# The expert stage of an attention and mixture-of-experts kernel: loops written out, two more row buffers, no copies of the index column

## The chip, the cores and the metric

The kernel runs on one core of one Trainium2 chip. The metric is the time of one execution on the device in microseconds (us), the median of several runs.

## What is computed

The reference takes `x` of shape (2, 1024, 256) and a context of shape (2, 154, 256), and makes two residual steps:

```python
x = x + attention(layernorm(x), ctx, Wq, Wkv, Wout, bout)      # 16 heads, causal past the context
x = x + ffn(layernorm(x), Wg, W1, W2)

def ffn(x, Wg, W1, W2):            # xt: 2048 tokens x 256, E = 8 experts, F = 512
    probs = softmax(xt @ Wg)
    top_idx = top_k(probs.T, T // E)          # each expert picks 256 tokens
    tok2exp = ...                             # one expert for each token
    weights = probs of that expert
    for e in range(E):
        gate = where(tok2exp == e, weights, 0)
        out = out + gate[:, None] * (gelu(xt @ W1[e]) @ W2[e])
```

Each token ends with exactly one expert, so the second step needs one pass of 2048 tokens through weights that depend on the token.

## The kernel before, in words

Five engines run programs of their own and meet at semaphores. Up to about 282 us the kernel does projections, attention and the gate's logits. Then the routing (282 to 326 us) finds each token's expert and sorts the tokens by expert into tiles of 128 slots. A tile holds tokens of one expert only, so some slots stay empty. Three tables say what is where: `slot_tok` [128, 24], column k of which holds the token numbers of tile k (a number past the last token for an empty slot); `slot_gate`, the weights; `r_texp`, the expert of each tile. 20 tiles (`NS_MOST`) are always done; 4 more only if the routing needed them (`more`), in a branch at the end of each engine's program.

The expert stage, which the change touches, does for each tile k:

1. GpSimd (POOL), `take`: an indirect DMA gathers 128 rows of `rows_d` (`token_rows` in the profile) by the token numbers into a row buffer `xs_sb` (part of the tensor `mid`). A row holds the normalised token (256 floats) and the residual (256 floats). There are `RING` = 4 row buffers, and one semaphore `xs_in` for each.
2. TensorE (PE), `ffn_xt`: two transposes of the normalised half to PSUM. ScalarE (ACT), `ffn_x`, copies them to SBUF.
3. ACT, `ffn_w`: reads the expert number from `r_texp` into a register and copies that expert's first-layer weights to one of two fixed buffers (`w1c_sb`, inside `piece_f`). PE, `ffn_w1`: 8 matmuls (16 records in the trace), first layer. ACT, `ffn_h`: gelu.
4. PE, `ffn_w2`: reads the expert number into a register of its own and does 4 matmuls (8 records) straight from the expert's second-layer weights, `w2_sb`.
5. VectorE (DVE), `ffn_y`: times the gate, plus the residual, into one of 4 buffers `y_sb`.
6. POOL, `give`: an indirect DMA scatters the 128 rows to `out`.

Called X(k) for `ffn_xt`, W1(k), W2(k), y(k), and take(k), give(k) below, the order on PE is X(0), W1(0), X(1), and then W1(k+1), X(k+2), W2(k) for each k. The order on POOL is the first four takes; then, when y(k) is done, take(k+4) into the buffer that y(k) has just read, and give(k). PE, ACT, DVE and POOL each run this as a hardware loop (`Fori`) whose body does four tiles. In a loop the column number k is a register, and the index operand of an indirect DMA is a fixed column, so POOL first copies column k to a small tensor with a `tensor_tensor` add of zero and waits for it on the semaphore `took`:

```python
nc.gpsimd.tensor_tensor(take_ix[u][:, :], slot_tok[:, bass.ds(k, 1)], zero1[:, :], ALU.add).then_inc(took, 1)
pool.wait_ge(took, at)
```

Of the kernel before, what the change touches and what calls it, by code (L numbers as in the profile page):

```python
# [44 lines left out]
RING = 4  # L45
NST = 3
# [63 lines left out]
def xattn_ffn(nc, x, ctx, Wq, Wkv, Wout, bout, Wg, W1, W2, out, rows_d, qd, kd, sums_d, recs_d, force_shift=False):  # L110
# [13 lines left out]
    with es:  # L124
# [107 lines left out]
        xs_in = [sem(f"xs_in{i}") for i in range(RING)]  # L232
# [75 lines left out]
        took = sem("took")  # L308
# [67 lines left out]
        xs_sb = [work(XW) for _ in range(RING)]  # L376
# [225 lines left out]
        def _(pool):  # L602
# [31 lines left out]
            nc.gpsimd.memset(zero1[:, :], 0).then_inc(tri_made, 1)  # L634
# [55 lines left out]
            def give(u, k, at):  # L690

                pool.wait_ge(fy_done, k + 1 + 2)
                nc.gpsimd.tensor_tensor(give_ix[u][:, :], slot_tok[:, bass.ds(k, 1)], zero1[:, :], ALU.add).then_inc(took, 1)  # L693
                pool.wait_ge(took, at)
                pool.sem_inc(index_there, 1)
                pool.indirect_dma_start(out_rows, bass.IndirectOffsetOnAxis(give_ix[u][:, :], 0), y_sb[u], None,  # L696
                                        bounds_check=T - 1, oob_is_err=False).then_inc(sent[u], 16)

            for u in range(RING):
                take(u, u, u + 1)  # L700
            for u in range(RING):
                pool.wait_ge(fy_done, u + 1 + 2)
                take(u, RING + u, RING + 2 * u + 1)
                give(u, u, RING + 2 * u + 2)
            with pool.Fori(1, NS_MOST // RING - 1) as it:
                for u in range(RING):
# [4 lines left out]
            at = 2 * NS_MOST - RING  # L711
            for u in range(RING):
                pool.wait_ge(sent[u], 16 * (NS_MOST // RING - 1))
                give(u, NS_MOST - RING + u, at + u + 1)
            pool.wait_ge(texp_done, 2)
            fl = pool.value_load(more[0:1, 0:1], min_val=0, max_val=1)
            with pool.If(fl > 0):
                with pool.Fori(NS_MOST // RING, NS // RING) as it:
                    for u in range(RING):
                        take(u, it * RING + u, it * (2 * RING) + u + 1)  # L720
                    for u in range(RING):
                        pool.wait_ge(sent[u], it * 16)
                        give(u, it * RING + u, it * (2 * RING) + RING + u + 1)
# [3 lines left out]
        def _(act):  # L727
# [135 lines left out]
            def ffn_w(pa, k):  # L863

                e = act.value_load(r_texp[0:1, bass.ds(k, 1)], min_val=0, max_val=E - 1)
                act.wait_ge(fh_ready, k + 1)
                nc.scalar.copy(w1c_sb[pa], w1_sb[:, bass.ds(e * (KT * F), KT * F)]).then_inc(fw_done, 1)  # L867

            def ffn_x(pa, k):
                act.wait_ge(fx_ready, k + 1)  # L870
                act.wait_ge(fh_ready, k + 1)
                nc.scalar.copy(xT_sb[pa], bank(pa)[:, 0:D]).then_inc(fx_done, 1)  # L872

            def ffn_h(pa, k):
                act.wait_ge(fh_ready, k + 1 + 2)
                act.wait_ge(fy_ready, k + 1)
                nc.scalar.activation(hT_sb[pa], bank(2 + pa), ACT.Gelu).then_inc(fg_done, 1)  # L877

            def tiles(k, last):
                for u in range(RING):  # L880
                    nxt = u < RING - 1 or not last
                    if nxt:
                        ffn_w((u + 1) % 2, k + u + 1)
                    ffn_h(u % 2, k + u)
                    if nxt:
                        ffn_x((u + 1) % 2, k + u + 1)

            ffn_w(0, 0)
            ffn_x(0, 0)
            with act.Fori(0, NS_MOST // RING - 1) as it:  # L890
                tiles(it * RING, False)
            tiles(NS_MOST - RING, True)
            fl = act.value_load(more[0:1, 0:1], min_val=0, max_val=1)
            with act.If(fl > 0):
                with act.Fori(NS_MOST // RING, NS // RING) as it:
                    ffn_w(0, it * RING)
                    ffn_x(0, it * RING)
                    tiles(it * RING, True)
# [3 lines left out]
        def _(pe):  # L902
# [276 lines left out]
            def ffn_xt(u, k, nth):  # L1179
# [546 lines left out]
```

## Time and profile before

| | |
|---|---|
| median of 3 runs | 428.44 us (428.04 to 429.25) |
| the profiled execution, its own time | 426.05 us |
| its span in the trace | 424.2 us |
| PE busy in the span | 359.4 us (85%) |
| ACT, DVE, POOL busy | 259.4, 208.5, 118.9 us |
| expert stage, first weight copy to last row out | about 327 to 424 us |

The span is what the trace covers; the execution's own time is 1.85 us longer. Engine time is counted as busy only while an instruction works; loading registers, branching and waiting is not. An indirect DMA on POOL is shown as busy for the time in which its descriptors are made; the data lands later.

### The profile page before, as it was taken

The page shows a single profiled execution, that of the slowest core. Times are in us where ns is not written, and L with a number is a line of the kernel's source. Part 1 is how long each engine was busy: PE and PEld are TensorE (multiplying, and loading weights), DVE is VectorE, ACT ScalarE, POOL GpSimd, SP SyncE. Part 2 cuts the span into 40 slices and gives each one's busy share as a digit, 9 for nine tenths or more (in the row PEclk, how much of TensorE's full clock was granted, in tenths as well). Part 3 has the DMA queues.
Part 4 walks back from the last instruction along what each step waited for, and adds up shares of the span by engine and source line. Part 5 has one row for each costly group of instructions (what it writes and reads, how often), then busy time and mean ns, then how long its engine had stood idle before and what let it go on. Part 6 is the DMA issues. An engine that isn't in the chain of part 4 may idle for free.

```text
span 424.2 us, 10996 instructions
## 1 busy us (share of the span) xinstructions
PE 359.4 (85%) x4207; PEld 232.5 (55%) x4208; DVE 208.5 (49%) x785; ACT 259.4 (61%) x354; POOL 118.9 (28%) x175
## 2 busy tenths in 40 slices
PE   2989898999999999999999999841139799989893
PEld 1646456445343545453435468830039788879782
DVE  5849973745373646363646558358877010101010
ACT  1456456899999999999999925430000444444430
POOL 4244789300030303030302100000001345555543
PEclk9999999899999999999999999555559999999999
DMA  8325995304494446434842352800000322222210
GB/s 271 97 102 154 275 272 167 125 4 101 112 258 113 105 117 201 118 98 126 235 122 39 94 182 96 287 15 1 0 2 2 93 64 76 65 81 68 76 50 26
DMA packets 36760, 47.61 MB, mean 112 GB/s; under 512 B 8460, under 2 KB 25794, under 8 KB 36705
## 3 DMA queue, kind: packets, MB, share of 16 engines
q1 hardware_dynamic: 33808, 40.26, 33.2%
q0 software_dynamic: 2560, 6.30, 5.0%
q8 instruction: 35, 0.57, 0.6%
q10 hardware_dynamic: 337, 0.32, 0.2%
q14 instruction: 20, 0.16, 0.1%
HBM read 32.71 MB, written 13.81 MB: 110 GB/s over the span
## 4 chain that ended last, share of the span: by engine, by line
PE 63%; DVE 13%; ACT 9%; DMA 6%; issue 5%; SPq 2%; POOL 1%; POOLq 0%; ACTq 0%; DVEq 0%
PE ps L1002 15%; PE ps L981 14%; PE ps L966 7%; PE ps L1204 7%; PE ps L1194 7%; ACT pbuf L790 6%; PE ps L950 4%; DVE v_st L1581 3%; PE ps L1091 2%; PE ps L1065 2%; DMA pbuf<-in_L_xattn_Wkv 2%; DMA mid<-token_rows,take_ix 2%; DMA sums<-mid 2%; PE ps L1082 1%; SPq L491 1%
## 5 line engine op out<-in xcount | busy, mean ns | idle before, releaser
L790 ACT ACTIVATE pbuf<-ps 128x1024 f32<-128x1024 f32 (+3 forms) x192 | 169.3, 1030 | 3.6 <-PE ps L981 3.5
L1454 DVE SCALAR_TENSOR_TENSOR pbuf<-pbuf,seen 128x128 f32<-128x128 f32 (+2 forms) x288 | 79.2, 317 | 64.1 <-ACT pbuf L790 63.6
L981 PE MATMUL ps<-q_st,k_st 98*32 98x512 bf16 (+4 forms) x2048 | 102.5, 320 | 3.1 <-ACT pbuf L790 2.6
L1002 PE MATMUL ps<-pbuf,v_st 128*32 128x512 f32 (+4 forms) x1024 | 97.8, 477 | 1.0 <-DVE pbuf L1454 0.9
L981 PEld LDWEIGHTS ps<-q_st,k_st 98*32 98x32 bf16 x2048 | 52.5, 96 | 69.8 <-ACT pbuf L790 27.1
L667 POOL TENSOR_TENSOR mid<-mid 64x1024 f32<-64x1024 f32 x7 | 16.6, 2370 | 126.7 <-DMA mid<-reciprocals 109.3
L867 ACT COPY piece_f<-wts 128x1024 f32 x20 | 20.9, 1045 | 48.8 <-DVE more L1669 45.0
L1682 DVE SCALAR_TENSOR_TENSOR mid<-ps,slot_gate,mid 128x256 f32<-128x256 f32 x20 | 9.7, 484 | 81.9 <-PE ps L1204 81.9
L1204 PE MATMUL ps<-wts,mid 128*128 x160 | 39.0, 387 | 4.9 <-ACT mid L877 3.2
L1002 PEld LDWEIGHTS ps<-pbuf,v_st 128*32 128x32 f32 x1024 | 27.5, 110 | 25.7 <-issue 11.8
L1194 PE MATMUL ps<-mid,piece_f 128*128 128x128 f32 x320 | 39.1, 275 | 1.2 <-ACT mid L872 0.7
L1194 PEld LDWEIGHTS ps<-mid,piece_f 128*128 128x128 f32 x320 | 38.7, 192 | 2.6 <-ACT mid L872 1.0
L877 ACT ACTIVATE mid<-ps 128x512 f32<-128x512 f32 x20 | 11.9, 597 | 41.2 <-PE ps L1194 41.2
L966 PE MATMUL ps<-mid,pbuf 128*128 128x512 f32 (+1 forms) x80 | 32.4, 547 | 4.9 <-ACT mid L755 3.5
L1204 PEld LDWEIGHTS ps<-wts,mid 128*128 128x128 f32 x160 | 28.9, 190 | 10.9 <-issue 7.6
L682 POOL TENSOR_TENSOR take_ix<-slot_tok,zero 128x1 uint32<-128x1 uint32 x20 | 3.9, 194 | 87.7 <-DVE slot_tok L1674 82.0
L685 POOL DMA_INDIRECT mid<-token_rows,take_ix x20 | 20.9, 1043 | 17.3 <-POOL take_ix L682 16.3
L696 POOL DMA_INDIRECT out<-mid,give_ix x20 | 20.3, 1015 | 18.7 <-POOL give_ix L693 14.5
L966 PEld LDWEIGHTS ps<-mid,pbuf 128*128 128x128 f32 x80 | 14.5, 196 | 17.9 <-issue 14.6
L1161 PE MATMUL ps<-cnt_b,same_e 128*128 128x3 bf16 x15 | 2.8, 187 | 22.8 <-DVE v_st L1581 22.8
L767 ACT CAST wts<-ps 128x512 bf16<-128x512 f32 (+1 forms) x20 | 10.4, 522 | 18.3 <-PE ps L966 18.3
L652 POOL TENSOR_TENSOR wts<-pbuf,wts 128x512 bf16<-128x512 f32 (+1 forms) x20 | 20.4, 1022 | 1.6
(215 smaller groups left out, 387.2 us busy)
## 6 DMA issues: line engine op xcount, KB each, us to landing
wts<-in_L_ffn_W SPq DMA_DIRECT2D x16, 512.0 KB, 4.9
k_st<-k_cut SPq DMA_DIRECT2D x48, 147.2 KB, 3.0
q_st<-q_cut SPq DMA_DIRECT2D x48, 128.0 KB, 2.9
q_cut<-wts SPq DMA_DIRECT2D x8, 384.0 KB, 3.6
k_cut<-wts SPq DMA_DIRECT2D x8, 384.0 KB, 4.2
xres<-in_x SPq DMA_DIRECT2D x4, 512.0 KB, 7.1
token_rows<-xres SPq DMA_DIRECT2D x4, 512.0 KB, 4.5
mid<-mid SPq DMA_DIRECT2D x28, 64.0 KB, 2.6
```

The lines of the kernel that those rows point to most:

```text
L652: nc.gpsimd.tensor_tensor(piece[:, i % NPIECES, 2, 0:w], rem[:, i % NREM, 0:w], piece[:, i % NPIECES, 1, 0:w], ALU.subtract).then_inc(low_ ...
L685: pool.indirect_dma_start(xs_sb[u], None, rows_d[:, :], bass.IndirectOffsetOnAxis(take_ix[u][:, :], 0), bounds_check=T - 1, oob_is_err=Fal ...
L696: pool.indirect_dma_start(out_rows, bass.IndirectOffsetOnAxis(give_ix[u][:, :], 0), y_sb[u], None, bounds_check=T - 1, oob_is_err=False).t ...
L790: nc.scalar.activation(pbuf[:, s % 2, r, c0:c1], st_ps[(s * GH + r) % NST][:, c0:c1], ACT.Exp, scale=SCALE).then_inc(exp_done, 1)
L867: nc.scalar.copy(w1c_sb[pa], w1_sb[:, bass.ds(e * (KT * F), KT * F)]).then_inc(fw_done, 1)
L950: last = nc.tensor.matmul(bk[:, i * D:(i + 1) * D], xcT[:, b, k, (t + i) * P:(t + i + 1) * P], wkv_sb[:, k, D:2 * D], start=(k == 0), stop ...
L966: last = nc.tensor.matmul(bk[:, 0:w], w_ap, xcT[:, b, k, c0:c0 + w], start=(k == 0), stop=(k == KT - 1))
L981: last = nc.tensor.matmul(st_ps[(s * GH + r) % NST][c:c + 32, a:z], k_st[pa][:, r, t * P + c:t * P + c + 32], q_st[pa][:, r, q0 + a - c0:q ...
L1002: last = nc.tensor.matmul(o_ps[32 * r:32 * r + 32, a:z], v_st[pa][:, t, r, :], pbuf[:, s % 2, r, a + dc:z + dc], start=(t == 0), stop=(t = ...
L1194: last = nc.tensor.matmul(bank(2 + pa)[:, c * P:(c + 1) * P], w1c_sb[pa][:, kk * F + c * P:kk * F + (c + 1) * P], xT_sb[pa][:, kk * P:(kk ...
L1204: last = nc.tensor.matmul(bank(6 + pa)[:, 0:D], hT_sb[pa][:, kk * P:(kk + 1) * P], w2_sb[:, bass.ds(e * (FT * D) + kk * D, D)], start=(kk ...
L1454: last = nc.vector.scalar_tensor_tensor(a, a, 3.0e38, seen[:, off:off + w], ALU.min, ALU.mult)
```

## The change

The `Fori` loops of the expert stage are gone on all four engines: the 20 tiles are written out, with constant column numbers. So `slot_tok[:, k:k + 1]` is given to the indirect DMAs directly, and `take_ix`, `give_ix`, `zero1` and the semaphore `took` are removed. There are `XRING` = 6 row buffers in place of 4: six takes are issued at the start, and then take(k+6) after y(k). The buffers `y_sb` stay at four. On PE the read of the expert number for W2(k) stands before W1(k+1), where before it stood between X(k+2) and W2(k). POOL's own wait for an earlier give (`sent`) is gone; DVE keeps its wait.

```diff
+XRING = 6
-        xs_in = [sem(f"xs_in{i}") for i in range(RING)]
+        xs_in = [sem(f"xs_in{i}") for i in range(XRING)]
-        xs_sb = [work(XW) for _ in range(RING)]
+        xs_sb = [work(XW) for _ in range(XRING)]
-        take_ix = [sb(f"take_ix{i}", [P, 1], U32) for i in range(RING)]
-        give_ix = [sb(f"give_ix{i}", [P, 1], U32) for i in range(RING)]
-        zero1 = sb("zero1", [P, 1], U32)
...
-            def take(u, k, at):
-
-                nc.gpsimd.tensor_tensor(take_ix[u][:, :], slot_tok[:, bass.ds(k, 1)], zero1[:, :], ALU.add).then_inc(took, 1)
-                pool.wait_ge(took, at)
+            def take(k):
+
                 pool.sem_inc(index_there, 1)
-                pool.indirect_dma_start(xs_sb[u], None, rows_d[:, :], bass.IndirectOffsetOnAxis(take_ix[u][:, :], 0),
-                                        bounds_check=T - 1, oob_is_err=False).then_inc(xs_in[u], 16)
+                pool.indirect_dma_start(xs_sb[k % XRING], None, rows_d[:, :], bass.IndirectOffsetOnAxis(slot_tok[:, k:k + 1], 0),
+                                        bounds_check=T - 1, oob_is_err=False).then_inc(xs_in[k % XRING], 16)
...
-            with pool.Fori(1, NS_MOST // RING - 1) as it:
-                for u in range(RING):
-                    pool.wait_ge(fy_done, it * RING + u + 1 + 2)
-                    take(u, it * RING + RING + u, it * (2 * RING) + RING + 2 * u + 1)
-                    pool.wait_ge(sent[u], it * 16)
-                    give(u, it * RING + u, it * (2 * RING) + RING + 2 * u + 2)
...
+            for k in range(XRING):
+                take(k)
+            for k in range(NS_MOST):
+                pool.wait_ge(fy_done, k + 1 + 2)
+                if k + XRING < NS_MOST:
+                    take(k + XRING)
+                give(k)
...
-            def ffn_w2(pa, k):
-                e = pe.value_load(r_texp[0:1, bass.ds(k, 1)], min_val=0, max_val=E - 1)
+            def ffn_w2(k, e):
+
                 pe.wait_ge(fg_done, k + 1 + 2)
                 pe.wait_ge(fy_done, k + 1)
...
+                for k in range(k0, k1):
+                    e = pe.value_load(r_texp[0:1, k:k + 1], min_val=0, max_val=E - 1)
+                    if k + 1 < k1:
+                        ffn_w1(k + 1)
+                    if k + 2 < k1:
+                        ffn_xt(k + 2)
+                    ffn_w2(k, e)
...
-                v.wait_ge(xs_in[u], nth)
-                if left is not None:
-                    v.wait_ge(sent[u], left)
-                nc.vector.scalar_tensor_tensor(y_sb[u], bank(6 + u % 2)[:, 0:D], slot_gate[:, bass.ds(k, 1)], xs_sb[u][:, D:XW],
-                                               ALU.mult, ALU.add).then_inc(fy_done, 1)
+                v.wait_ge(xs_in[k % XRING], 16 * (k // XRING + 1))
+                if k >= RING:
+                    v.wait_ge(sent[k % RING], 16 * (k // RING))
+                nc.vector.scalar_tensor_tensor(y_sb[k % RING], bank(6 + k % 2)[:, 0:D], slot_gate[:, k:k + 1],
+                                               xs_sb[k % XRING][:, D:XW], ALU.mult, ALU.add).then_inc(fy_done, 1)
```

On POOL, one tile of the loop before (a register computation is an ISA or REGISTER_ALU row):

```order
L682 ISA [waits fy_done]
L682 TENSOR_TENSOR take_ix0<-slot_tok,zero1 128x1
L683 ISA
L685 DMA mid<-token_rows,take_ix0 128x512 [waits took]
L709 REGISTER_ALU
L693 ISA [waits fy_done,sent0]
L693 TENSOR_TENSOR give_ix0<-slot_tok,zero1 128x1
L694 REGISTER_ALU
L696 DMA out_0<-mid,give_ix0 2048x256 [waits took]
```

And POOL after the change, from the last instruction of the attention part (L663) through the first six takes to the first pair:

```order
L663 TENSOR_TENSOR mid<-mid 64x1024 [waits packed,den_in,v_in,scaled]
L679 DMA mid<-token_rows,slot_tok 128x512 [waits lg_ready,rows_sent,scaled,idx_done]
L679 DMA mid<-token_rows,slot_tok 128x512 x5
L679 DMA mid<-token_rows,slot_tok 128x512 [waits fy_done]
L688 DMA out_0<-mid,slot_tok 2048x256 [waits fy_done]
```

A tile's two DMAs now stand directly behind each other, with no vector instruction and no wait for one between them.

On PE, one tile of the loop before: first layer (L1194), transposes (L1184), the read of the expert number (L1200), second layer (L1204):

```order
L1194 MATMUL ps<-mid,piece_f 128x128 [waits fg_done,fx_done,fw_done]
L1194 MATMUL ps<-mid,piece_f 128x128 x7
L1184 MATMUL ps<-ident,mid 128x128 [waits fx_done,xs_in3]
L1184 MATMUL ps<-ident,mid 128x128
L1200 TENSOR_LOAD r_texp
L1200 ISA x2
L1204 ISA [waits fy_done,fg_done]
L1204 MATMUL ps<-wts,mid 128x256
```

The same tile after the change, where these are L1170, L1159, L1194 and L1180:

```order
L1194 TENSOR_LOAD r_texp
L1194 ISA x2
L1170 MATMUL ps<-mid,piece_f 128x128 [waits fg_done,fx_done,fw_done]
L1170 MATMUL ps<-mid,piece_f 128x128 x7
L1159 MATMUL ps<-ident,mid 128x128 [waits fx_done,xs_in3]
L1159 MATMUL ps<-ident,mid 128x128
L1180 ISA [waits fy_done,fg_done]
L1180 MATMUL ps<-wts,mid 128x256
```

The read has moved from behind the wait for the gathered rows (`xs_in3`) to ahead of the first layer; one register row is left between the transposes and the second layer.

## Rows read from the trace of the kernel before

**Rows 1.** Timeline, PE, first tiles: start us, us, engine line operation

```profile
337.67 1.89 PE L1204 MATMUL ps<-wts,mid 128*128 x8
339.40 1.95 PE L1194 MATMUL ps<-mid,piece_f 128*128 128x128 f32 x16
341.18 0.38 PE L1184 MATMUL ps<-ident,mid 128*128 128x128 f32 x2
341.40 1.89 PE L1204 MATMUL ps<-wts,mid 128*128 x8
```

**Rows 2.** Timeline, PE and ACT, later tiles; in brackets the idle time before

```profile
366.93 1.89 PE L1204 MATMUL ps<-wts,mid 128*128 x8
...
370.99 0.43 PE L1184 MATMUL ps<-ident,mid 128*128 128x128 f32 x2 [0.39 <-DMA mid<-token_rows,take_ix]
...
372.19 1.99 PE L1204 MATMUL ps<-wts,mid 128*128 x8 [0.76 <-issue]
...
376.49 0.37 ACT L872 COPY mid<-ps 128x256 f32<-128x256 f32 x1
...
377.91 1.95 PE L1194 MATMUL ps<-mid,piece_f 128*128 128x128 f32 x16
```

**Rows 3.** Timeline, the last two tiles on PE, DVE and POOL

```profile
413.81 3.62 PE L1204 MATMUL ps<-wts,mid 128*128 x16
...
417.56 0.99 POOL L696 DMA_INDIRECT out<-mid,give_ix  x1 [0.88 <-POOL give_ix L693]
417.58 0.48 DVE L1682 SCALAR_TENSOR_TENSOR mid<-ps,slot_gate,mid 128x256 f32<-128x256 f32 x1 [1.23 <-PE ps L1204]
418.58 0.20 POOL L693 TENSOR_TENSOR give_ix<-slot_tok,zero 128x1 uint32<-128x1 uint32 x1
419.66 0.99 POOL L696 DMA_INDIRECT out<-mid,give_ix  x1 [0.88 <-POOL give_ix L693]
```

**Rows 4.** Timeline, POOL, one tile of the loop

```profile
366.40 0.20 POOL L682 TENSOR_TENSOR take_ix<-slot_tok,zero 128x1 uint32<-128x1 uint32 x1
...
367.46 1.03 POOL L685 DMA_INDIRECT mid<-token_rows,take_ix  x1 [0.86 <-POOL take_ix L682]
...
368.52 0.20 POOL L693 TENSOR_TENSOR give_ix<-slot_tok,zero 128x1 uint32<-128x1 uint32 x1
...
369.63 1.02 POOL L696 DMA_INDIRECT out<-mid,give_ix  x1 [0.91 <-DVE mid L1682]
...
370.68 0.20 POOL L682 TENSOR_TENSOR take_ix<-slot_tok,zero 128x1 uint32<-128x1 uint32 x1
```

**Rows 5.** Line L685, the 20 takes, from issue to landing

```profile
DMA to landing us min/median/max: 2.2/3.4/3.6
```

**Rows 6.** Line L1200, PE's sequencer reading the expert number, ns min/median/max

```profile
L1200 PEldq FUSED_REGOPS  x36: 37/151/156, 335.9 to 413.2; - x36
L1200 PEldq TENSOR_LOAD <-r_texp x20: 297/308/538, 335.9 to 412.9; - x20
```

**Rows 7.** Chain that ended last, around the first take

```profile
326.63 0.20 POOL take_ix L682
...
326.98 0.86 issue
327.84 3.58 DMA mid<-token_rows,take_ix
```

**Rows 8.** Chain that ended last: POOL's sequencer issues the take of rows 4

```profile
366.74 0.51 issue
```

**Rows 9.** Busy time by stretch: length, PE, PEld, DVE, ACT, POOL, PEclk, DMA share, GB/s

```profile
372.20:393.70 21.50, 19.93 (x131) 17.83 (x131) 2.42 (x5) 9.60 (x15) 12.02 (x21) 1.00 0.25 73
```

**Rows 10.** DMA queues of the whole span and of 326 to 424 us: packets, MB, share

```profile
q8 instruction: 35, 0.57, 0.6%
...
q8 instruction: 4, 0.07, 0.3%
```

**Rows 11.** The attention stage's first matmul line on the page: busy, mean ns, idle before

```profile
L981 PE MATMUL ps<-q_st,k_st 98*32 98x512 bf16 (+4 forms) x2048 | 102.5, 320 | 3.1 <-ACT pbuf L790 2.6
```

More of the change, by code:

```diff
@@ L307, in xattn_ffn @@
         idx_done = sem("idx_done")
-        took = sem("took")
         index_there = sem("index_there")
@@ L711, in _ @@
[L711 to L714, printed above, removed]
+                pool.indirect_dma_start(out_rows, bass.IndirectOffsetOnAxis(slot_tok[:, k:k + 1], 0), y_sb[k % RING], None,
+                                        bounds_check=T - 1, oob_is_err=False).then_inc(sent[k % RING], 16)
+            for k in range(XRING):
[5 more added lines that the diff above has]
+                give(k)
@@ L717, in _ @@
             with pool.If(fl > 0):
[L718 to L723, printed above, removed]
+                for k in range(NS_MOST, NS):
+                    take(k)
+                for k in range(NS_MOST, NS):
+                    give(k)
         @blk.scalar
@@ L879, in tiles @@
[L879 to L892, printed above, removed]
+                nc.scalar.activation(hT_sb[k % 2], bank(2 + k % 2), ACT.Gelu).then_inc(fg_done, 1)
@@ L893, in _, with tiles @@
+            def tiles(k0, k1):
+                ffn_w(k0)
+                ffn_x(k0)
+                for k in range(k0, k1):
+                    if k + 1 < k1:
+                        ffn_w(k + 1)
+                    ffn_h(k)
+                    if k + 1 < k1:
+                        ffn_x(k + 1)
+            tiles(0, NS_MOST)
             fl = act.value_load(more[0:1, 0:1], min_val=0, max_val=1)
             with act.If(fl > 0):
[L895 to L898, printed above, removed]
+                tiles(NS_MOST, NS)
@@ L1203, in ffn_w2 @@
                 for kk in range(FT):
-                    last = nc.tensor.matmul(bank(6 + pa)[:, 0:D], hT_sb[pa][:, kk * P:(kk + 1) * P],
+                    last = nc.tensor.matmul(bank(6 + k % 2)[:, 0:D], hT_sb[k % 2][:, kk * P:(kk + 1) * P],
                                             w2_sb[:, bass.ds(e * (FT * D) + kk * D, D)], start=(kk == 0), stop=(kk == FT - 1))
@@ L1210, in _, with tiles @@
             pe.wait_ge(texp_done, 2)
-            def first(k, nth):
-                ffn_xt(0, k, nth)
-                ffn_w1(0, k)
-                ffn_xt(1, k + 1, nth)
-            def tiles(k, nth, last):
-                for u in range(RING):
-                    if u + 1 < RING or not last:
-                        ffn_w1((u + 1) % 2, k + u + 1)
-                    if u + 2 < RING or not last:
-                        ffn_xt((u + 2) % RING, k + u + 2, nth if u + 2 < RING else nth + 16)
-                    ffn_w2(u % 2, k + u)
-            first(0, 16)
-            with pe.Fori(0, NS_MOST // RING - 1) as it:
-                tiles(it * RING, it * 16 + 16, False)
-            tiles(NS_MOST - RING, 16 * (NS_MOST // RING), True)
+            def tiles(k0, k1):
+                ffn_xt(k0)
+                ffn_w1(k0)
+                ffn_xt(k0 + 1)
+                for k in range(k0, k1):
+                    e = pe.value_load(r_texp[0:1, k:k + 1], min_val=0, max_val=E - 1)
+                    if k + 1 < k1:
+                        ffn_w1(k + 1)
+                    if k + 2 < k1:
+                        ffn_xt(k + 2)
+                    ffn_w2(k, e)
+            tiles(0, NS_MOST)
             fl = pe.value_load(more[0:1, 0:1], min_val=0, max_val=1)
             with pe.If(fl > 0):
-                with pe.Fori(NS_MOST // RING, NS // RING) as it:
-                    first(it * RING, it * 16 + 16)
-                    tiles(it * RING, it * 16 + 16, True)
+                tiles(NS_MOST, NS)
         @blk.vector
@@ L1692, in _ @@
             with v.If(fl > 0):
-                with v.Fori(NS_MOST // RING, NS // RING) as it:
-                    for u in range(RING):
-                        ffn_y(u, it * RING + u, it * 16 + 16, it * 16)
+                tiles(NS_MOST, NS)
 _INS = ["x", "ctx_1024", "L0_xattn_Wq", "L0_xattn_Wkv", "L0_xattn_Wout", "L0_xattn_bout",
```

53 lines of the change are left out of this document (20 added, 33 removed).

## The prediction

> **What bounds the stage now.** I read the timeline of PE first, since the chain that ended last is nearly all PE in this stage. The reader should see in [rows 1] what a tile costs when nothing is late: W2(0) starts at 337.67 and W2(1) at 341.40, so W2, W1 and X stream through PE in 3.73 us: W2 takes 339.40 - 337.67 = 1.73, W1 341.18 - 339.40 = 1.78 and X 341.40 - 341.18 = 0.22. The whole stage is slower. W2(0) starts at 337.67 [rows 1] and W2(18) at 413.81 in a row that holds the last two tiles [rows 3]. These are 18 steps in 76.14 us. Streaming they would be 17 of 3.73 and one without X of 3.51 (there is no X(20)), 66.92 us. So 9.22 us of the stage is time in which PE had nothing to do.
>
> [Rows 2] show how it is lost, in the worst step, W2(7) at 366.93 to W2(8) at 372.19, 5.26 us: PE waits for the gathered rows until 370.99, does X(10), and then stands another 0.76 us before W2(8), which the view calls issue. The rows were gathered by the take at 367.46 [rows 4], and [rows 7] show 3.58 us and [rows 5] a median of 3.4 us from such an issue to landing: 367.46 + 3.4 = 370.9. The 0.76 is the read of the expert number: its load takes 0.30 us and more, and a register computation of 0.15 follows [rows 6], with waits and one more computation ahead of the first W2 matmul. PE's sequencer runs ahead of the array, but it can't pass X while X's rows are missing, so the read starts only when they land.
>
> Next, why the takes are late. [Rows 4] show POOL through one tile: copy at 366.40, take at 367.46, copy at 368.52, give at 369.63, next copy at 370.68. This is 4.28 us per tile, 0.55 more than PE's 3.73, and nothing in it waits for another engine for long: copy 0.20, then 0.86, DMA 1.03, copy 0.20, then 0.91, DMA 1.02. POOL is busy for only 12.02 of 21.50 us in [rows 9], but its gaps are the copies' completion and the start of the next DMA. So POOL paces the stage, and it reaches PE through the landing of the rows. Four buffers leave it no room. y(k) is done about 1.73 + 0.65 = 2.4 us after W2(k) starts (the last W2 ends at 413.81 + 3.62 = 417.43, its y at 418.06 [rows 3]), and X(k+4) is due 2 x 3.73 - 0.22 = 7.2 us after it, which leaves 4.8 us; the take needs 0.2 + 0.86 + 3.4 = 4.5 plus what POOL is behind.
>
> ACT and DVE aren't near a limit: in 21.50 us, five tiles, ACT works 9.60 and DVE 2.42 [rows 9]. The tightest path through ACT is gelu, then the copy of X, then the next W1: that copy ended at 376.49 + 0.37 = 376.86 and the W1 behind it began at 377.91 [rows 2], 1.05 us later, in a step without a PE gap. The granted clock is 1.00 there, the 2.4 GHz level [rows 9].
>
> **The change, part by part.**
>
> *No index copies.* A tile loses two vector instructions (2 x 0.20) and their completion. What a DMA then costs on POOL isn't in the trace. From above: each still needs the 0.86 or 0.91 ahead of it, so 0.88 + 1.03 + 0.03 between instructions, twice, 3.9 us. From below: the sequencer needs 0.51 us to issue one [rows 8] and may do so while the previous one works, so 1.03 + 0.03, twice, 2.1 us. I take about 3.3, nearer the upper row, because part of the 0.86 is certainly the start of the DMA. All three are below 4.28. At 3.9 POOL would fall behind PE by 0.17 per tile, 2.4 us over the 14 tiles with takes, which the next part covers.
>
> *Six buffers.* X(k+6) is due 4 x 3.73 - 0.22 = 14.7 us after W2(k) starts, 12.3 after y(k). The take needs 4.5, so rows land some 7.8 us early, where now there is 0.3. The first six takes last at most 6 x 1.94 = 11.6 us from 326.9 to 338.5, before y(0) is done at about 340, so they delay nothing. y(k) still needs its y buffer back from give(k-4); that was issued four tiles, 14.9 us, earlier. With this no X waits for rows: PE streams, and the gain is the whole 9.22, down to 9.22 - 1.5 if a few tiles are still disturbed.
>
> *The earlier read of the expert number.* It now stands behind W2(k-1), with 1.73 us of queued matmuls as cover, against some 0.76 to 1.0 of need. In its old place it has W1 and X as cover, 2.0 us, once rows are on time, and [rows 1] show that this is enough: W2(1) follows X at once. So it is worth 0 by itself beside six buffers. If the cover failed it would cost 0.76 per tile; that is a rival below.
>
> *No loops.* PE's back edge falls between two tiles behind queued matmuls, and POOL's register rows overlap a DMA. I count nothing for either.
>
> *Start.* The first take waits for its copy: 326.63 to 326.98 is the copy and its completion [rows 7]. That goes, -0.3 us, and the chain from there to W2(0) shifts with it. The bounds are 0 and 0.35.
>
> *End.* The last y ends at 417.58 + 0.48 = 418.06. Its give starts at 419.66, because the copy waited until the give before had finished, 417.56 + 0.99 = 418.55 [rows 3]. Without copies the give before starts and ends 0.3 earlier, and the last starts about 0.1 + 0.86 after y, 419.0: -0.65 us, bounds 0.3 and 0.9.
>
> *Instruction supply.* The program is longer: the trace shows 35 packets of instructions for 0.57 MB, 16 KB each, four of them in the expert stage [rows 10]. That is 0.3% of 16 x 98 us, 1.2 us each. The Trainium skill's page "Runtime: NRT & Kernel Launch", section "Instruction fetch mechanics", states that an engine streams straight-line code in blocks of 16 KiB (256 instructions), mostly hidden, and that a taken branch outside the held window stalls. The packet size agrees; that it is hidden is borne out by the next row. In attention PE executes 2048 matmuls of one line with 3.1 us idle before them, 2.6 of it waiting for ACT [rows 11], in written-out code that needs instructions far faster than this stage. By the page's count 16 further tiles of about 56 instructions would be an estimated three or four blocks and cost nothing. I count nothing either, and a rival prices the opposite.
>
> **The sum**, against the profiled execution: 9.2 + 0.3 + 0.65 = 10.2 us, 426.05 - 10.2 = 415.9. The median of the runs is 2.4 us above that execution, so in its terms 428.44 - 10.2 = **418.2 us**. About 0.3% (1.3 us) is what can be told from no change here.
>
> **The rivals.**
>
> *A. PE streams* (forecast), 418.2; its own range is 416.5 to 420. Chance 0.74.
>
> *B. Partly.* Something still holds PE: blocks of instructions that arrive late (PE, POOL and ACT, 4 to 5 more crossings of 1.2 us, 5 to 6 us on the path), or a POOL at its upper bound together with DMAs that take longer with six in flight. The gain is 4 to 7, 421.5 to 424.5. For it: written-out loops do need more blocks [rows 10]. Against it: [rows 11], and 7.8 us of slack on each gather. Chance 0.17.
>
> *C. No change.* POOL stays at 4.28 because the time ahead of each DMA isn't the copy's but its own and grows to fill it, for instance because a column of a wide table is slower to read than a small tensor. It would take 0.2 us more for each DMA. Two further buffers then only defer the lag by two tiles: 14 takes behind a 0.55 us deficit are 7.7 us, and the slack is 7.8, so even then most of the gain stays; only at 0.5 us more for each DMA is nearly nothing left: a deficit of 1.2 over 14 tiles, less 7.8, loses 9 of the 10.2. 427 to 429.5. Chance 0.04.
>
> *D. Slower: the early read stalls W1.* If PE's array has run dry by the time that the sequencer comes to the read, the read stands in front of W1 in each tile. It needs 0.76 in [rows 2], up to 1.0 with its waits. 19 times that is 14 to 19 us, less the 10.2 gained: 432 to 437. It decides from 10.2 / 19 = 0.54 us of uncovered time per tile. Against it: it sits behind 1.73 us of W2, whose eight records are queued at once, and the W1 wait for the copy of X comes 1.05 us before W1 is due [rows 2]. Chance 0.05.
>
> **How the numbers follow.** Faster is A and B, 0.91, and a little of C, 0.92; same is 0.03; slower is D, 0.05. The range from 416.0 (A with all terms at their best and 0.2% of scatter) to 423.5 leaves out the upper end of B, C and D.
>
> **What would show it.** Right: in the timeline W2 to W2 is 3.73 us in nearly all steps and 66.9 us from W2(0) to W2(18); no X waits for a DMA and no W2 for issue; POOL waits for DVE in each tile, and its pair of DMAs lasts 2.1 to 3.9 us; the first take starts at about 327.5 of its old scale; the last give starts 1 us after the last y. Wrong: gaps ahead of W1 (D), X still waiting for takes whose spacing is over 3.73 (C), or gaps at a few fixed places with instruction packets beside them (B).

## The result, and the profile after

The changed kernel took 422.49 us (median of 4 runs, 420.46 to 423.21), against 428.35 us for the kernel before (4 runs, 428.04 to 429.25). The ratio is 0.9852, interval 0.9813 to 0.9891. It is faster by 5.9 us, or 1.5%, where 10.2 us were forecast. The profiled execution took 423.04 us (span 421.1), against 426.05 of the one before, 3.0 less. The same file was measured twice more, on two different chips, beside the experiments below: 417.50 us (ratio 0.9766, 0.9721 to 0.9811) and 417.46 us (ratio 0.9750, 0.9721 to 0.9779). There the gain was 10.4 and 10.0 us. So there are two things to explain: why the gain is 10, and where some 4.3 us of it went in the first measurement. (A ratio leaves out executions that were over 1.5% slower than the kernel's fastest, at a lower granted clock; that concerns two of the six runs of f4 alone.)

The steady part first, from the timeline of the changed kernel (start, duration, engine, line, operation, out<-in, count, and in brackets the idle time before and what ended it):

```profile
351.61 1.04 POOL L679 DMA_INDIRECT mid<-token_rows,slot_tok  x1 [1.42 <-DVE mid L1652]
352.05 1.89 PE L1180 MATMUL ps<-wts,mid 128*128 x8
352.95 1.01 POOL L688 DMA_INDIRECT out<-mid,slot_tok  x1 [0.31 <-issue]
353.78 1.95 PE L1170 MATMUL ps<-mid,piece_f 128*128 128x128 f32 x16
...
355.57 0.38 PE L1159 MATMUL ps<-ident,mid 128*128 128x128 f32 x2
355.78 1.89 PE L1180 MATMUL ps<-wts,mid 128*128 x8
```

This answers to [rows 2] and [rows 4]. PE has no idle time in front of X or W2, and W2 follows W2 in 355.78 - 352.05 = 3.73 us. All 17 steps that contain an X are 3.73, the last is 3.51. The page has no idle time ahead of any of the 20 second layers (busy us, mean ns, idle us), where the kernel before had 4.9:

```profile
L1180 PE MATMUL ps<-wts,mid 128*128 x160 | 37.7, 379 | 0.0
```

POOL's pair is take 351.61, give 352.95, done at 353.96, so 2.35 us from start to end, and then POOL waits for DVE's y. Its gap ahead of the give is 0.31 us, where [rows 4] had a copy and 0.91. Now the end, the counterpart of [rows 3], the last two tiles on PE and the last two on POOL:

```profile
411.54 3.62 PE L1180 MATMUL ps<-wts,mid 128*128 x16
...
414.86 0.98 POOL L688 DMA_INDIRECT out<-mid,slot_tok  x1 [2.53 <-DVE mid L1652]
415.20 0.48 DVE L1652 SCALAR_TENSOR_TENSOR mid<-ps,slot_gate,mid 128x256 f32<-128x256 f32 x1 [1.24 <-PE ps L1180]
416.58 0.98 POOL L688 DMA_INDIRECT out<-mid,slot_tok  x1 [0.75 <-issue]
```

W2(18) starts at 411.54 and W2(0) started at 344.59 (below): 66.95 us, where the kernel before has 76.14. The last give starts 416.58 - 415.68 = 0.90 us after the last y.

The start is where the loss is. The same view, from the first take to W2(0), to be read beside [rows 1]:

```profile
328.92 1.26 POOL L679 DMA_INDIRECT mid<-token_rows,slot_tok  x1 [82.83 <-DVE slot_tok L1644]
330.49 1.01 POOL L679 DMA_INDIRECT mid<-token_rows,slot_tok  x1 [0.31 <-issue]
...
332.65 0.41 PE L1159 MATMUL ps<-ident,mid 128*128 128x128 f32 x2 [0.45 <-DMA mid<-token_rows,slot_tok]
...
335.74 1.01 POOL L679 DMA_INDIRECT mid<-token_rows,slot_tok  x1 [0.30 <-issue]
336.30 0.37 ACT L853 COPY mid<-ps 128x256 f32<-128x256 f32 x1 [6.81 <-remote]
...
336.77 3.01 PE L1170 MATMUL ps<-mid,piece_f 128*128 128x128 f32 x16 [3.70 <-issue]
...
340.78 3.75 PE L1170 MATMUL ps<-mid,piece_f 128*128 128x128 f32 x16 [0.57 <-issue]
...
344.59 1.89 PE L1180 MATMUL ps<-wts,mid 128*128 x8
```

X(0) is done at 333.06, but ACT's copy of it starts only at 336.30, 3.65 us after X(0) started. In the kernel before this was 0.44. ACT had been idle for 6.81 us, so it is not ACT that was late but the signal that it waited for. PE then stands idle for 3.70 us, and W1(0) and W1(1) last 3.01 and 3.75 us where they take 1.95 later. The windows of those stretches (us of the stretch, busy time and count of PE, weight loads, DVE, ACT and POOL, then the granted clock, the DMA share and GB/s) say why:

```profile
332.20:336.70 4.50, 0.42 (x3) 0.21 (x2) 0.00 (x0) 0.37 (x1) 3.58 (x4) 1.00 0.65 175
...
336.70:340.70 4.00, 3.44 (x18) 3.06 (x18) 0.00 (x0) 1.90 (x3) 0.04 (x1) 0.61 0.27 84
340.70:344.60 3.90, 3.82 (x19) 3.85 (x20) 0.00 (x0) 1.08 (x2) 0.00 (x0) 0.52 0.00 0
344.60:348.30 3.70, 3.70 (x28) 3.49 (x27) 0.48 (x1) 1.87 (x3) 0.45 (x1) 1.00 0.02 4
```

In the 4.5 us before, PE worked for 0.42. After that the granted clock is 0.61 and then 0.52, that is most and then nearly all of the time at 1.2 GHz, and only from 344.6 on is it 1.00 again, 2.4 GHz. From W1(0) to W1(1) it is 4.01 us where the kernel before has 2.97, and from W1(1) to W2(0) 3.81 where it has 2.11.

So this execution accounts for itself: -9.19 in the steady part, -0.35 from the slot table to the first take, -0.81 at the end, + 3.21 + 1.04 + 1.70 = 5.95 for the late copy and the low clock, -0.10 for rows that land sooner, and +1.43 because the slot table itself was later than in the profile before (327.75 against 326.32), ahead of anything that the change touches. The sum is -3.1, and the two spans differ by 3.1.

### The profile page after: what moved, and what is told of

Its sections match the earlier page's. It is cut to its first block, busy times and chain, and to the rows that moved or that the text cites. A ratio compares the mean times of both kernels' runs of the same rounds, so it can differ in the third digit from the quotient of the medians.

```text
span 421.1 us, 10732 instructions
## 1 busy us (share of the span) xinstructions
PE 358.9 (85%) x4207; PEld 235.2 (56%) x4207; DVE 207.3 (49%) x785; ACT 259.1 (62%) x353; POOL 110.6 (26%) x134
## 4 chain that ended last, share of the span: by engine, by line
PE 67%; DVE 14%; ACT 9%; issue 4%; SPq 3%; DMA 3%; POOL 0%; POOLq 0%; DVEq 0%; ACTq 0%
PE ps L978 14%; PE ps L957 13%; PE ps L1170 9%; PE ps L942 8%; PE ps L1180 8%; ACT pbuf L771 7%; PE ps L926 4%; DVE v_st L1551 3%; DVE pbuf L1424 3%; PE ps L1067 2%; PE ps L1041 2%; SPq L488 2%; DMA pbuf<-in_L_xattn_Wkv 2%; PE ps L1058 1%; PE ps L1130 1%
## 5 line engine op out<-in xcount | busy, mean ns | idle before, releaser
L978 PE MATMUL ps<-pbuf,v_st 128*32 128x512 f32 (+4 forms) x1024 | 96.8, 473 | 1.9 <-DVE pbuf L1424 1.7
L679 POOL DMA_INDIRECT mid<-token_rows,slot_tok x20 | 20.8, 1039 | 113.4 <-DVE slot_tok L1644 82.8
L663 POOL TENSOR_TENSOR mid<-mid 64x1024 f32<-64x1024 f32 x7 | 16.6, 2370 | 126.7 <-DMA mid<-reciprocals 126.7
L1170 PE MATMUL ps<-mid,piece_f 128*128 128x128 f32 x320 | 41.8, 287 | 4.3 <-issue 4.3
L1170 PEld LDWEIGHTS ps<-mid,piece_f 128*128 128x128 f32 x320 | 41.2, 202 | 5.8 <-issue 4.9
L942 PE MATMUL ps<-mid,pbuf 128*128 128x512 f32 (+1 forms) x80 | 34.1, 570 | 4.9 <-ACT mid L736 3.5
L1180 PE MATMUL ps<-wts,mid 128*128 x160 | 37.7, 379 | 0.0
L1180 PEld LDWEIGHTS ps<-wts,mid 128*128 128x128 f32 x160 | 28.9, 190 | 3.1
L688 POOL DMA_INDIRECT out<-mid,slot_tok x20 | 20.1, 1005 | 17.2 <-DVE mid L1652 12.2
L748 ACT CAST wts<-ps 128x512 bf16<-128x512 f32 (+1 forms) x20 | 10.4, 522 | 20.0 <-PE ps L942 20.0
L646 POOL CAST wts<-pbuf 128x512 bf16<-128x512 f32 (+1 forms) x20 | 11.0, 552 | 28.8 <-DVE pbuf L1373 28.8
```

What stands on the lines that cost most here:

```text
L679: pool.indirect_dma_start(xs_sb[k % XRING], None, rows_d[:, :], bass.IndirectOffsetOnAxis(slot_tok[:, k:k + 1], 0), bounds_check=T - 1, oo ...
L942: last = nc.tensor.matmul(bk[:, 0:w], w_ap, xcT[:, b, k, c0:c0 + w], start=(k == 0), stop=(k == KT - 1))
L978: last = nc.tensor.matmul(o_ps[32 * r:32 * r + 32, a:z], v_st[pa][:, t, r, :], pbuf[:, s % 2, r, a + dc:z + dc], start=(t == 0), stop=(t = ...
L1170: last = nc.tensor.matmul(bank(2 + k % 2)[:, c * P:(c + 1) * P], w1c_sb[k % 2][:, kk * F + c * P:kk * F + (c + 1) * P], xT_sb[k % 2][:, kk ...
L1180: last = nc.tensor.matmul(bank(6 + k % 2)[:, 0:D], hT_sb[k % 2][:, kk * P:(kk + 1) * P], w2_sb[:, bass.ds(e * (FT * D) + kk * D, D)], star ...
```

## The experiments

All start from the changed kernel and compute the whole output. e1 to e4 ran on one chip, e5 to e8 on a second, f1 to f4 on a third; the kernel before had 427.86 us (7 runs), 427.90 (13) and 427.46 (11) there. Differences are against these.

All stretches come from the timelines, as differences of two starts (us), to about 0.01. The "take0" column is the first take to X(0), the last one W2(18) to the last give:

| kernel | take0 to X(0) | X(0) to its copy | W1(0) to W2(0) | W2(0) to W2(18) | to last give |
|---|---|---|---|---|---|
| before | 3.83 | 0.44 | 5.08 | 76.14 | 5.85 |
| after, first measurement | 3.73 | 3.65 | 7.82 | 66.95 | 5.04 |
| e8, the changed kernel again | 5.80 | 0.43 | 5.10 | 66.95 | 5.04 |
| e1, takes held | 5.83 | 0.43 | 5.10 | 66.95 | 5.04 |
| e2, PE kept running | 5.93 | 2.80 | 5.08 | 66.95 | 5.04 |
| e3, four buffers | 5.34 | 0.66 | 5.10 | 67.42 | 5.04 |
| e4, copies back | 3.80 | 0.45 | 5.10 | 66.95 | 7.00 |
| e5, late read | 3.79 | 0.45 | 5.10 | 66.95 | 5.04 |
| e6, four buffers and copies | 3.99 | 0.42 | 5.10 | 74.47 | 5.73 |

### Which part brings the 9.2 us: e3, e4, e6

e3 keeps the changed kernel and goes back to four buffers:

```diff
-XRING = 6
+XRING = 4
```

> The changed kernel with four row buffers in place of six, so four back-to-back takes. Theory 1 (back-to-back gathers cause the delay) expects a shorter or equal delay of X(0), since four gathers are over sooner: 0 to 3.2 us. In the steady part a take needs 0.7 + 3.4 of the 4.8 us that are left, so it streams at 3.73 with little or no loss: 420 to 423. If the six buffers were what made it stream, the W2-to-W2 step is over 3.9 and the time 426 or more.

Measured: 418.50 us (416.10 to 421.05), ratio 0.9778 (0.9709 to 0.9847). The steady part is 67.42. Of its 18 steps one is 4.15 and one 3.78, where X is just late:

```profile
358.05 1.89 PE L1180 MATMUL ps<-wts,mid 128*128 x8
...
361.31 1.04 POOL L679 DMA_INDIRECT mid<-token_rows,slot_tok  x1 [1.38 <-DVE mid L1652]
...
361.93 0.44 PE L1159 MATMUL ps<-ident,mid 128*128 128x128 f32 x2 [0.20 <-DMA mid<-token_rows,slot_tok]
```

From W2(k) to the take behind y(k) it is 361.31 - 358.05 = 3.26 us here, and with the 3.4 of [rows 5] 6.7 us of the 7.2 until X is due. So four buffers are nearly enough once POOL has no copies to make: what the last two add is 0.5 us in the trace.

e4 keeps six buffers and puts the copies back, in straight code with constant columns:

```diff
+            def index(ix, k):
+                nc.gpsimd.tensor_tensor(ix, slot_tok[:, k:k + 1], zero1[:, :], ALU.add).then_inc(took, 1)
+                copies[0] += 1
+                pool.wait_ge(took, copies[0])
             def take(k):
+                index(take_ix[k % XRING], k)
...
                 pool.wait_ge(fy_done, k + 1 + 2)
+                index(give_ix[k % RING], k)
```

> The changed kernel with the index copies put back (written out, six buffers). POOL needs 4.28 us per tile again, and the first takes are 2.1 us apart. Theory 1 expects no delay of X(0). The lag of 0.55 us per tile is covered by the slack of 7.8 us for 14 takes, so PE still nearly streams, and the last give is 0.65 us later: about 418. If the copies were what bound the stage in spite of the buffers: 424 or more.

Measured: 418.27 us (417.37 to 421.35), ratio 0.9786 (0.9723 to 0.9849). The steady part is 66.95, the same as without copies. What POOL is behind shows only at the end, in the timeline of e4 (the last two tiles):

```profile
404.56 3.62 PE L1195 MATMUL ps<-wts,mid 128*128 x16
...
408.22 0.48 DVE L1667 SCALAR_TENSOR_TENSOR mid<-ps,slot_gate,mid 128x256 f32<-128x256 f32 x1 [1.24 <-PE ps L1195]
...
409.46 1.00 POOL L703 DMA_INDIRECT out<-mid  x1 [0.88 <-DVE mid L1667]
...
411.56 0.99 POOL L703 DMA_INDIRECT out<-mid  x1 [0.88 <-POOL mid L685]
```

The last y is done at 408.70 and its give starts at 411.56, 2.86 us later in place of 0.90: POOL is two us behind. It fell behind by up to 0.55 us a tile while there were takes, the two further buffers kept that from PE, as rival C of the prediction had worked out for another cause, and six tiles with gives alone (409.46 to 411.56, 2.1 us each) made up for part of it. So in the trace the removal of the copies is worth 2.0 us at the end beside six buffers, and the 0.35 us ahead of the first take; nothing in between. The medians of e1, e3 and e4, from one chip, can't part it from nothing.

e6 takes both away. What stays of the change is the code written out and the early read of the expert number:

```diff
-XRING = 6
+XRING = 4
...
+                index(take_ix[k % XRING], k)
...
+                index(give_ix[k % RING], k)
```

> Loops written out and the early read, but four row buffers and the index copies as before the change. My account of the gain (POOL's 4.28 us per tile reaching PE through four buffers) expects W2(0) to W2(18) near 76 us and 426 to 428 in all. If the loops themselves, or the place of the read, carried part of the gain, it is under 424.

Measured: 425.16 us (10 runs, 423.27 to 429.26), ratio 0.9957 (0.9925 to 0.9988). The steady part is 74.47, 1.7 below that of before. Its timeline around X(5), and one line of its table of waits (engine, what it works on, what it waited for: us in all, times, longest), from W2(0) on:

```profile
343.08 0.20 POOL L685 TENSOR_TENSOR mid<-slot_tok,zero 128x1 uint32<-128x1 uint32 x1
...
344.15 1.04 POOL L693 DMA_INDIRECT mid<-token_rows,mid  x1 [0.87 <-POOL mid L685]
...
347.37 0.20 POOL L685 TENSOR_TENSOR mid<-slot_tok,zero 128x1 uint32<-128x1 uint32 x1
...
347.60 0.44 PE L1174 MATMUL ps<-ident,mid 128*128 128x128 f32 x2 [0.17 <-DMA mid<-token_rows,mid]
347.88 1.94 PE L1195 MATMUL ps<-wts,mid 128*128 x8
```

```profile
PE ps L1174 <- DMA mid<-token_rows,mid: 4.8, 9, 1.6
```

POOL's period is 347.37 - 343.08 = 4.29 us, as in [rows 4], so written-out code gives POOL nothing, and X waits for its rows again. But W2 follows X at once, 347.60 to 347.88, where [rows 2] had another 0.76 us. So this third part of the change isn't worth 0 when rows are late: about 1.7 us in the trace, 2.7 in the medians.

The experiment doesn't part the read from the loops. The trace of the kernel before says what filled the gap: between X(10) at 370.99 and W2(8) at 372.19 stands the load of the expert number (ns; start us).

```profile
L1200 PEldq TENSOR_LOAD <-r_texp x1: 517/517/517, 371.1 to 371.1; - x1
```

In the kernel before W2 starts up to 1.20 us after its X, in e6 never more than 0.28. Over the 18 tiles the difference is some 6.5 us, and only 1.7 of it comes back, because POOL's 4.29 us a tile still set when rows land.

Put together: without the copies, four buffers lose only 0.5 us; with six buffers, the copies lose only the 2.0 us at the end; with four buffers and copies, 7.5 of the 9.2 us are lost. The two parts aren't terms of a sum. They are two covers for one lag, and either is nearly enough.

### The early read: e5

```diff
                 for k in range(k0, k1):
-                    e = pe.value_load(r_texp[0:1, k:k + 1], min_val=0, max_val=E - 1)
                     if k + 1 < k1:
                         ffn_w1(k + 1)
                     if k + 2 < k1:
                         ffn_xt(k + 2)
+                    e = pe.value_load(r_texp[0:1, k:k + 1], min_val=0, max_val=E - 1)
```

This was made on e1, whose hold of the takes is described below.

> The changed kernel with the takes held as in the first of these experiments (two, then four more after the copy of X(0)), and the read of the expert number back between X(k+2) and W2(k). If that read is covered by W1 and X once rows are on time, every step from W2 to W2 stays 3.73 us and the time is that of the held version, 417 to 419.5. If the early read was worth something by itself, steps are 3.9 or more and the time 421 or more.

Measured: 417.44 us (416.27 to 419.36), ratio 0.9762 (0.9708 to 0.9817). Its timeline has the same steps, and W2 follows X without a gap:

```profile
380.27 1.89 PE L1182 MATMUL ps<-wts,mid 128*128 x8
...
383.78 0.38 PE L1161 MATMUL ps<-ident,mid 128*128 128x128 f32 x2
...
384.00 1.89 PE L1182 MATMUL ps<-wts,mid 128*128 x8
```

384.00 - 380.27 = 3.73. Once rows are on time the place of the read is worth nothing.

### The late copy of X(0): e1, e2, e7, e8, f1, f2

The theory after the first result: six gathers in a row hold back PE's signal. Then a train that is cut should bring the signal at once. e1 lets two takes go and waits for the copies of X(0) before the others:

```diff
             for k in range(XRING):
+                if k == 2:
+                    pool.wait_ge(fx_done, 3)
                 take(k)
```

> The changed kernel, but POOL issues only two takes at the start and waits for the copy of X(0) before the other four. The profile of the changed kernel shows X(0)'s semaphore arriving 3.2 us after its matmuls, and then W1(0) and W1(1) at the 1.2 GHz clock. Theory 1, the six back-to-back gathers cause the delay: X(0) to W1(0) is about 0.9 us as before the change, the clock stays at 1.00, W2(0) starts about 9.8 us after the first take, and the time falls by 5.9 us from the changed kernel's, to about 416.6. Theory 2, the delay has another cause (the written-out code or the place of the read): it stays, 422.5.

Measured: 419.31 us (416.98 to 422.22), ratio 0.9802 (0.9730 to 0.9873). The copy comes 0.43 us after X(0), and the clock is not lost.

e2 leaves the train as it is and fills PE's idle time, so that the clock should stay at 2.4 GHz:

```diff
                 ffn_xt(k0)
+                if k0 == 0:
+                    keep_running(60)
                 ffn_w1(k0)
```

> The changed kernel with 60 extra small matmuls (results unused) between X(0) and W1(0), 3.4 us of work for PE. If only X(0)'s signal is late and PE itself is free, the fillers run at once, the clock stays at the 2.4 GHz level, and W1(0) and W1(1) take back 1.0 and 1.7 us: about 419.8. If PE itself is held, the fillers come after the hold, and the kernel is 3 us slower than the changed one.

Measured: 422.95 us (422.40 to 424.32), ratio 0.9884 (0.9834 to 0.9935). The timeline of e2:

```profile
334.52 0.39 PE L1159 MATMUL ps<-ident,mid 128*128 128x128 f32 x2
334.75 1.47 PE L1130 MATMUL ps<-same_e,ones_b 128*128 128x128 bf16 x19
335.41 1.01 POOL L679 DMA_INDIRECT mid<-token_rows,slot_tok  x1 [0.31 <-issue]
...
337.20 2.45 PE L1130 MATMUL ps<-same_e,ones_b 128*128 128x128 bf16 x41 [0.99 <-issue]
...
337.32 0.37 ACT L853 COPY mid<-ps 128x256 f32<-128x256 f32 x1 [8.61 <-remote]
...
339.49 2.00 PE L1170 MATMUL ps<-mid,piece_f 128*128 128x128 f32 x16
```

The clock part of the theory holds: W1(0) lasts 2.00 us, not 3.01, and the 2.7 us of low clock are gone. But the copy is late again, 337.32 - 334.91 = 2.4 us after the end of X(0), and the fillers, which wait for nobody, stand still too for 0.99 us just before. It is PE that is held, not only its signal. It doesn't wait for instructions that arrive late, the cause in the prediction's rival B: instruction packets start at 327.64 and then 347.76 in the first measurement's trace, at 326.91 and 338.76 in that of e2, none of them in the hold. Most of what the fillers save they cost themselves (1.7 of 2.7 us): W1(0) comes 2.17 us after the start of the copy in place of 0.47.

On this evidence the train looked guilty: late in both kernels with six takes in a row, not in e1, nor in e4 (takes 2.1 us apart, by its copies), and 0.2 us late in e3 (four in a row). e7 waits for take(0)'s rows before take(1), and e8 is the changed kernel unaltered, the control:

```diff
             for k in range(XRING):
+                if k == 1:
+                    pool.wait_ge(xs_in[0], 16)
                 take(k)
```

> The changed kernel, but take(1) and the further ones wait until the rows of take(0) have landed. X(0) then runs before the burst's transfers start. If the transfers of the burst hold X(0), there is no hold, X(0)'s signal comes 0.4 us after its start, and the time is 417 to 419.5, unless X(1) becomes late: its rows land 3.6 + 0.9 + 3.4 = 7.9 us after take(0), X(0) to W1(1) takes 3.9, so W1(1) starts about 0.7 us late. If the hold needs only POOL making descriptors behind it, it appears again at X(1): 421 or more.

> The changed kernel itself once more, for its startup. If the hold of X(0) belongs to six back-to-back takes, the signal of X(0) is again 2 us or more late, and the time is 421 to 423.5. If it was a chance of one execution, W2(0) starts 9.8 us after the first take and the median is near 417.

Measured: e7 416.90 us (416.00 to 419.34), ratio 0.9757 (0.9700 to 0.9813), though its second take is late and W1(1) comes 1.1 us later for it; e8 417.50 (416.49 to 418.40), ratio 0.9766 (0.9721 to 0.9811). The control took the theory down. Its timeline has the same six takes in a row, and no late copy:

```profile
324.71 7.58 PE L1130 MATMUL ps<-same_e,ones_b 128*128 128x128 bf16 x89
...
326.33 1.26 POOL L679 DMA_INDIRECT mid<-token_rows,slot_tok  x1 [82.76 <-DVE slot_tok L1644]
...
332.13 0.39 PE L1159 MATMUL ps<-ident,mid 128*128 128x128 f32 x2
332.56 0.37 ACT L853 COPY mid<-ps 128x256 f32<-128x256 f32 x1 [6.23 <-PE ps L1159]
...
333.03 2.02 PE L1170 MATMUL ps<-mid,piece_f 128*128 128x128 f32 x16 [0.51 <-issue]
```

On the third chip stand the control once more (f1) and a hold (f2: as e7, but with `k == 2`, so that two takes go ahead):

> The changed kernel a third time, beside its held version on the same chip. It has been measured at 422.5 with X(0)'s signal 3.2 us late, and at 417.5 with the signal on time. If the hold is a property of the six-take burst on some chips, this run is either about 5 us above the held version or equal to it, and its profile shows which. If it is chance from execution to execution, its runs spread from 416 to 424.

> The changed kernel, where POOL issues take(0) and take(1), waits until the rows of take(0) have landed, and then issues the other four. X(0) runs before the transfers of the four; X(1)'s rows land in time. Theory 1 (the burst holds X(0)): 416.5 to 418 on any chip. Theory 2 (the burst has nothing to do with it): the same time as the unchanged one of this call.

Measured: f1 417.46 us (6 runs, 415.54 to 418.22), ratio 0.9750 (0.9721 to 0.9779); f2 416.73 (6 runs, 415.44 to 419.98), ratio 0.9751 (0.9714 to 0.9788). No late copy in either. The hold brings nothing that can be told from nothing. What stays: the late copy was seen in two profiles out of five with six takes in a row (after, e2; not e8, f1, f3), and in none of the eight others, but for the 0.2 us in e3. So the train is not sufficient for it; whether it is necessary, and what else it takes, is open.

One rival stands untested, the chip or the way in which it was recorded. Every late copy, the 0.2 us of e3 too, is in the first measurement or on the chip of e1 to e4, and the unaltered kernel never ran there beside e1. These five profiles also differ in their recording: each gather sends 16 landing signals, 320 for the 20 takes, and the nine other traces hold all 320, but those of after and e1 to e4 hold 251, 268, 252, 274 and 178. A loss of records isn't enough for a late copy either, since e4 has the fewest and its copy is on time. So e1 shows a start without the hold, not that its wait cured it.

The first measurement's four runs (420.46 to 423.21) and the ten of e8 and f1 (415.54 to 418.40) don't overlap, while the kernel before moved by 0.9 us between all of them, which fits a loss that comes or stays away for a whole measurement.

### The fillers ahead of X(0): f3, f4

In e8 above X(0) starts at 332.13, 5.80 us after the first take, and 3.7 in the first measurement. In front of it stand the 90 filler matmuls of `keep_running`, which are to keep the clock up; they last 5.19 us there, and here the 89 in view 7.58. The windows of e8 and, below it, of the kernel before (columns as above):

```profile
324.70:332.20 7.50, 7.50 (x92) 7.50 (x91) 0.46 (x3) 1.04 (x1) 4.65 (x5) 0.66 0.32 95
```

```profile
326.00:331.60 5.60, 4.77 (x86) 4.60 (x83) 0.47 (x5) 1.05 (x1) 2.87 (x5) 1.00 0.20 50
```

With a granted clock of 0.66 the fillers end after the rows have landed, and X(0) waits some 2 us for them. It is so in e1, e2, e3, e8 and f1, whose W1(0) then lasts 2.00 to 2.02 us. In after, e4, e5, e7 and f2, with the same 90 fillers, they last 5.19 (in e6 6.20), so both cases occur in one kernel. The one profile of the kernel before is of the short kind; whether it too has the long one at times isn't known. f3 has fewer fillers, f4 the same with f2's hold:

```diff
-            keep_running(90)
+            keep_running(50)
```

> The changed kernel with 50 instead of 90 filler matmuls ahead of X(0). In the traces so far the 90 end 4.2 us after the token table where the clock is at 2.4 GHz, before the rows land, but 6.9 us after it where they begin at 1.2 GHz, and X(0) is then 2 us late. With 50 they end at the latest 4.8 us after the table, so X(0) never waits for them: the mean falls by 0.5 to 1.5 us and the spread of the runs narrows. Against: PE stands idle for up to 2.7 us ahead of X(0), and W1(0) and W1(1) may then run at 1.2 GHz, which costs 2.7 us: 1 to 2 us slower.

> Both together. If both effects are as I think, the fastest version: 415.5 to 417. If fewer fillers cost the clock, 418 to 420.

Measured: f3 417.63 us (6 runs, 414.02 to 420.01), ratio 0.9758 (0.9716 to 0.9800); f4 416.72 (6 runs, 414.12 to 422.14), ratio 0.9716 (0.9678 to 0.9754). The timeline of f3:

```profile
327.83 5.12 PE L1130 MATMUL ps<-same_e,ones_b 128*128 128x128 bf16 x50
329.53 1.26 POOL L679 DMA_INDIRECT mid<-token_rows,slot_tok  x1 [83.90 <-DVE slot_tok L1644]
...
333.40 0.41 PE L1159 MATMUL ps<-ident,mid 128*128 128x128 f32 x2 [0.45 <-DMA mid<-token_rows,slot_tok]
...
333.85 0.37 ACT L853 COPY mid<-ps 128x256 f32<-128x256 f32 x1 [4.33 <-PE ps L1159]
...
334.32 2.02 PE L1170 MATMUL ps<-mid,piece_f 128*128 128x128 f32 x16 [0.51 <-issue]
```

The fillers take 5.12 us for 50, 0.10 each, at a granted clock of 0.55 (50 take 2.95 us at 1.00 in f4); but now X(0) waits for its rows, 3.87 us after the take, and W1(0) keeps 2.02 us. The profile has the 2 us back, the medians don't: 417.63 against 417.46 for f1. f4 has the lowest ratio of all, 0.35% under f1 and f2, but the intervals overlap, and its median over all six runs is f2's. It is no proven gain.

## Why the prediction was right, and what it missed

**The steady stage** (term 9.22) measured 9.19: W2(0) to W2(18) is 66.95 us in place of 66.92 forecast, in every profile of the unaltered change. Steps of 3.73, no X waiting for a DMA, no W2 waiting for issue, POOL waiting for DVE in each tile: each sign is there. PE is the only limit left in this stretch. e6 confirms the account of the loss as well: with copies and four buffers back POOL turns in 4.29 us and 7.5 us of it return.

**No index copies.** "I take about 3.3, nearer the upper row" was too high. Takes in a row are 1.31 us apart, take and give 1.34, and the pair lasts 2.35 us, near the lower end. The reason given for it didn't hold, "because part of the 0.86 is certainly the start of the DMA": behind another DMA only 0.31 of gap stays, so most of the 0.86 is either the copy's or is done while the DMA before works. No run tells which. It cost the forecast nothing, since 2.35 and 3.3 are both below 3.73.

**Six buffers.** The statement that rows land long before they are due holds. That the gain rests on them doesn't: e3 keeps 8.7 of the 9.2 with four.

**The earlier read** is worth 0 beside six buffers, as stated (e5). Rival D, the read stalling W1, did not happen: W1 has no gap in any steady step. **No loops**, "I count nothing", stands for the whole change too. As long as rows are late, e6 has the two together at about 1.7 us, and the trace puts that on the read.

**Start** and **end** (0.3 and 0.65) measured 0.35 and 0.81. Of the end, 2.0 us would have been lost with six buffers and copies (e4). The bounds held both.

**Instruction supply.** The page's row of instruction packets after the change, beside [rows 10]:

```profile
q8 instruction: 38, 0.62, 0.6%
```

Three packets more (38 against 35) and 0.05 MB, the low end of the three or four blocks estimated from the page "Runtime: NRT & Kernel Launch", section "Instruction fetch mechanics", of the Trainium skill. By that page of the Trainium skill the cost of crossing into the next block is mostly hidden, and the trace agrees: no step of the steady stage is longer than 3.73 us.

**What was missed** is the start of the stage. The working says of the first six takes that "they delay nothing", and asked of them only whether they are done before y(0). The first measurement's profile lost 5.95 us between X(0) and W2(0): 3.2 by the late copy, 2.7 by the granted clock that PE lost in the 3.7 us that it stood idle. Rival B had the right size (a gain of 4 to 7) by the wrong causes: no instruction packet falls into the hold, and X(0)'s rows came 3.73 us after their take, no later than before. That the first measurement's 422.49 lies inside the range given is owed to the room left for B; the forecast's own range ended at 420. Without the hold the kernel takes 417.50 and 417.46 us, near the 418.2 forecast, and there is some luck in that too: in the profile of e8 the start carries a loss of 2.0 us behind the fillers that the sum didn't have, and it is partly offset by a slot table that comes 1.16 us earlier than in the profile before, ahead of the change. The step that failed is "they delay nothing", the start priced by the takes alone. In the two tiles before W2(0) no queue of matmuls covers PE: whatever delays one signal there is paid in full, and again in clock.

The clock part is shown, by e2, which took 2.7 us of it away, in a profile whose copy was late as well. The origin of the held signal is not. The train of gathers was the theory, and the repeats without the hold refute it as a sufficient cause.

## What to carry to other kernels

A late gather can be covered by more buffers or by a shorter turn of the queue that issues it, and either may do: the second one then measures as nearly nothing, so try each alone before keeping both. Price an operation in a train of its own kind by start-to-start intervals, not by adding up the gap that it shows when it stands alone. And measure the unaltered kernel again beside every repair of a startup loss, on the same chip: here the control, not the repairs, told how much there was to repair, and it is missing on the one chip where the loss was seen again.

## What the runs showed of the hardware

- An indirect DMA of 128 rows keeps POOL busy for 1.01 us, and the next may start 0.31 us later, 1.31 us from start to start (behind the first one 1.57). A lone one after a copy on POOL waits 0.85 to 0.91 us. Its index may be one column of a wide table: the first take lands no later (3.73 to 3.87 us to X(0), where the fillers don't hold it) than with a small tensor (3.83).
- The 90 filler matmuls last 5.19 us at a granted clock of 1.00 in one execution (after), and 89 of them 7.58 us at 0.66 in another of the same kernel (e8). This alone moves X(0) by 2 us.
- In one execution (after) a stretch of 3.7 us with PE idle was followed by 7.9 us at a granted clock of 0.61 and 0.52, with PE busy for 7.3 of them.
- PE can stand still for 1 us in a run of matmuls that wait for nothing (e2), at the end of six gathers in a row. The cause is open.
- A read of the expert number that PE's sequencer makes between two matmul groups costs nothing when the group ahead runs without a wait (e5, 3.73 us a step), and 0.76 us of idle PE when it waits for its rows (the kernel before).
